# First router: additions between the statistics, the shared expert in front of each group's logits with a sigmoid, the first pair's missing weights spread by TensorE

## The reference, cut to what matters

```python
logits = x @ router_w.T + expert_bias[None, :]
probs = jax.nn.sigmoid(logits)
top_w, top_idx = jax.lax.top_k(probs, 8)
top_w = top_w / (jnp.sum(top_w, axis=-1, keepdims=True) + 1e-09) * 2.5
combine = zeros((T, 160)).at[arange(T)[:, None], top_idx].set(top_w)
h1 = jax.nn.silu(jnp.einsum('th,eih->eti', x, w_gate))
routed = jnp.einsum('eti,ehi->th', h1 * combine.T[:, :, None], w_down)
shared = jax.nn.silu(x @ w_gate_shared.T) @ w_down_shared.T
return routed + shared
```

## Time and profile before

| | us |
|---|---|
| median of 3 runs | 1087.96 |
| lowest and highest | 1087.72 and 1097.57 |
| the profiled execution | 1088.41 |
| its span in the trace | 1086.4 |
| PE, DVE, ACT, POOL busy | 1022.1, 821.4, 801.1, 227.5 |
| loop over heads ends, first mixture's loop starts | 316.2 and 365.2 |

### The profile page before, as it was taken

One profiled execution on the slowest core, in us unless ns is written; L12 is line 12 of the kernel. 1 busy time (PEld: TensorE's weight loads), 2 busy tenths in 40 slices (PEclk: granted clock), 3 DMA queues, 4 the chain that ended last, 5 costly groups with the idle time before them and its releaser, 6 DMA issues.

```text
span 1086.4 us, 20393 instructions
## 1 busy us (share of the span) xinstructions
PE 1022.1 (94%) x5232; PEld 692.5 (64%) x5264; DVE 821.4 (76%) x1954; ACT 801.1 (74%) x1326; POOL 227.5 (21%) x337
## 2 busy tenths in 40 slices
PE   5799999999987799999999999999999998799998
PEld 3333333333344588888888888888866777587786
DVE  8544444444439499999999999999986886799897
ACT  6699999999964677777777777888864443266664
POOL 3777764555452000000000000000023112000000
PEclk9999999999998999999999999999999998899999
DMA  4478787667650677777777777777720000223321
GB/s 139 127 234 263 242 258 227 215 228 229 223 169 5 223 257 248 242 241 242 240 242 234 247 239 242 241 241 238 236 73 1 1 1 1 81 86 117 122 81 39
DMA packets 103419, 190.51 MB, mean 175 GB/s; under 512 B 11980, under 2 KB 56652, under 8 KB 103372
## 3 DMA queue, kind: packets, MB, share of 16 engines
q1 hardware_dynamic: 103380, 190.06, 53.9%
HBM read 154.03 MB, written 35.98 MB: 175 GB/s over the span
## 4 chain that ended last, share of the span: by engine, by line
PE 84%; DVE 6%; ACT 3%; issue 2%; DMA 2%; POOL 2%; SPq 0%; DVEq 0%; ACTq 0%; POOLq 0%
PE bank L1348 27%; PE bank L1361 16%; PE bank L1203 11%; PE bank L1355 8%; PE bank L1184 6%; PE bank L1187 5%; PE bank L1450 2%; PE bank L1214 1%; PE bank L1434 1%; DVE xn L1541 1%; POOL m_norm L815 1%; DMA ring<-c_rows 1%; DVE stats L1529 1%; PE bank L1139 1%; ACT silu_z L1042 1%
## 5 line engine op out<-in xcount | busy, mean ns | idle before, releaser
L1348 PE MATMUL bank<-xh,w_parts 128*128 128x512 f32 x896 | 276.3, 390 | 1.6 <-DVEq L1757 1.6
L928 ACT ACTIVATE ring<-bank,minus_bound 128x1024 f32<-128x1024 f32 x256 | 262.8, 1119 | 9.2 <-DVE bank L1638 6.2
L1016 ACT ACTIVATE bank<-bank 128x512 f32<-128x512 f32 x320 | 186.2, 582 | 89.2 <-PE bank L1348 89.2
L1771 DVE TENSOR_TENSOR bank<-bank,ring 128x512 f32<-128x512 f32 x320 | 223.8, 699 | 27.8 <-DMA ring<-c_rows 2.9
L1361 PE MATMUL bank<-hh,w_parts 128*128 128x512 f32 x776 | 239.3, 389 | 0.0
L1763 DVE TENSOR_TENSOR hl<-bank,hh 128x512 fp32r<-128x512 f32 x321 | 218.2, 680 | 0.1
L1010 ACT ACTIVATE hh<-bank 128x512 fp32r<-128x512 f32 x321 | 190.5, 594 | 2.6 <-DVE bank L1771 2.4
L1348 PEld LDWEIGHTS bank<-xh,w_parts 128*128 128x128 f32 x896 | 167.4, 188 | 37.4 <-DVEq L1757 1.8
L1638 DVE TENSOR_TENSOR bank<-bank,corner 128x128 f32<-128x128 f32 x256 | 76.3, 298 | 151.8 <-PE bank L1187 149.3
L1348 PE MATMUL bank<-xl,w_parts 128*128 128x512 f32 x448 | 174.4, 389 | 0.0
L1361 PEld LDWEIGHTS bank<-hh,w_parts 128*128 128x128 f32 x776 | 145.6, 188 | 30.7 <-ACT hh L1010 0.4
(11 more groups left out here) (297 smaller groups left out, 1131.6 us busy)
## 6 DMA issues: line engine op xcount, KB each, us to landing
ring<-c_rows SPq DMA_DIRECT2D x176, 512.0 KB, 4.7
w_parts<-w_pairs SPq DMA_DIRECT2D x160, 128.0 KB, 2.9
w_pairs<-xh SPq DMA_DIRECT2D x16, 768.0 KB, 4.4
q_stack<-q_parts SPq DMA_DIRECT2D x64, 144.0 KB
k_stack<-k_parts SPq DMA_DIRECT2D x192, 48.0 KB
w_pairs<-xl SPq DMA_DIRECT2D x16, 512.0 KB, 2.9
big<-in_w_exp SPq DMA_DIRECT2D x16, 384.0 KB, 4.9
w_ffn_parts<-xl SPq DMA_DIRECT2D x16, 384.0 KB, 3.8
```

The source lines that it names most:

```text
L928: act.activation(ring[:, c % RING * S:(c % RING + 1) * S], wide[(m + c) % SB][:], ACT.Exp, bias=minus_bound[:]).then_inc(exp_done, 1)
L1016: act.activation(bank(4 + c % ZB), bank(4 + c % ZB), ACT.Silu).then_inc(silu_ready, 1)
L1348: ins = pe.matmul(out_, w[i], x_[j], start=start and k == 0, stop=stop and k == 2, skip_group_check=not start)
L1771: dve.tensor_tensor(bank(4 + c % ZB), bank(4 + c % ZB), cb[u][:, g * GW:(g + 1) * GW], ALU.mult).then_inc(hid_ready, 1)
```

## The change

It has four parts. PE's first two projections stand inside both branches of the If, ahead of its end. DVE adds a projection ahead of that group's statistics, and not all four first. The shared expert's first product stands ahead of each group's logits; ACT takes from it a copy (`shared_z`) and a sigmoid (`shared_hid`), and POOL multiplies the two, so that no Silu is left ahead of the loop; the four spare matmuls per group are gone, and the second product stands behind the first group's turned weights. For the last group DVE scales the weights, ACT copies both parts, and for the first pair of experts PE spreads the rows of tokens 1024 to 2047 with a matrix of ones and zeros (`pair_rows`), which ACT copies to the place that a load filled before.

```diff
--- before.py
+++ after.py
@@ -173,6 +173,7 @@
         b_rest = sb("b_rest", [P, NE])
         bias_rows = sb("bias_rows", [P, NE], F32R)
         ones_r = sb("ones_r", [P, P], F32R)
+        pair_rows = sb("pair_rows", [P, P])
         w_shared = sb("w_shared", [P, EI])
         wd_shared = sb("wd_shared", [EI, D])
         gates = big[:, 2 * T:2 * T + NT * NE].rearrange("p (t e) -> p t e", t=NT)
@@ -211,6 +212,7 @@
 
         act_out = [q_stack[0][u][:].bitcast(F32) for u in range(2)]
         shared_hid = act_out + [k_stack[0][u][:].bitcast(F32) for u in range(2)]
+        shared_z = [k_stack[1][u][:].bitcast(F32) for u in range(2)] + [evac[u][:] for u in range(2)]
         hid = [q_stack[1][u][:].bitcast(F32) for u in range(2)]
         hh = [sb(f"hh{u}", [P, GW], F32R) for u in range(2)]
         hl = [sb(f"hl{u}", [P, GW], F32R) for u in range(2)]
@@ -593,14 +597,13 @@
                 load_pair(u, u)
             for g in range(G):
                 cols = slice(g * GW, (g + 1) * GW)
-                sp.wait_ge(cT_ready, min(2 * g + 2, 2 * G - 1))
-                if g == G - 1:
-                    sp.wait_ge(cT_end, 1)
+                sp.wait_ge(cT_ready, 2 * g + 1)
                 sp.dma_start(c_dram[0:P, cols], cT_first[:, cols]).then_inc(c_saved, 16)
+                sp.wait_ge(cT_ready, 2 * g + 2)
                 sp.dma_start(c_dram[P:NE, cols], cT_last[:, cols]).then_inc(c_saved, 16)
                 if g % 2:
                     sp.wait_ge(c_saved, 2 * (g + 1) * 16)
-                    for u in range(2):
+                    for u in range(g // 2, 2):
                         load_rows(u, u, g // 2)
             for u in range(2, CB):
                 for h in range(2):
@@ -771,6 +774,9 @@
 
             pool.wait_ge(w1_loaded, 4 * 16)
             link(pool.tensor_copy(ones_r[:], ones[:]))
+            for e in range(2):
+                link.sign(pool.tensor_copy(pair_rows[:, e:P:2], across(ident[:, e:e + 1], EI)))
+            link.wait()
             link(pool.tensor_copy(b_part[0][:], b_router[:]))
             link(pool.tensor_tensor(b_rest[:], b_router[:], b_part[0][:].bitcast(F32), ALU.subtract))
             link(pool.tensor_copy(b_part[1][:], b_rest[:]))
@@ -786,6 +792,9 @@
             link(pool.memset(hid[1], 0.0))
             pool.sem_inc(moe_zero, 1)
             norm(1)
+            for g in range(G):
+                pool.wait_ge(shared_act, g + 1)
+                pool.tensor_tensor(shared_hid[g][0:EI], shared_hid[g][0:EI], shared_z[g][0:EI], ALU.mult).then_inc(shared_ready, 1)
             link(pool.memset(v_flat[:, 0:NT * 2 * B * NCH], 0.0))
             for h in range(2):
                 link.sign(pool.memset(half_column(h, 2, 0, NT), 1.0 / CH))
@@ -970,36 +979,42 @@
 
             def take_group(g):
 
+                act.wait_ge(shared_psum, g + 1)
+                act.activation(shared_z[g][0:EI], bank(2 + g % 2)[0:EI, :], ACT.Copy)
+                act.activation(shared_hid[g][0:EI], bank(2 + g % 2)[0:EI, :], ACT.Sigmoid).then_inc(shared_act, 1)
                 take_logits(g)
                 high_x(g, 1)
 
-            def take_shared(g):
-
-                act.wait_ge(shared_psum, g + 1)
-                act.activation(shared_hid[g][0:EI], bank(2 + g % 2)[0:EI, :], ACT.Silu).then_inc(shared_act, 1)
-
             act.wait_ge(w_saved[0], 16 + NH // 2 * 16)
+            act.wait_ge(moe_zero, 1)
             norm(1, take_group)
             take_group(G - 1)
-            act.wait_ge(moe_zero, 1)
 
             def take_cT(g):
 
                 cols = slice(g * GW, (g + 1) * GW)
                 act.wait_ge(cT_psum, g + 1)
                 act.activation(cT_first[:, cols], bank(4 + g % 2), ACT.Copy).then_inc(cT_ready, 1)
+                act.activation(cT_last[:, cols], bank(6 + g % 2)[0:NE - P, :], ACT.Copy).then_inc(cT_ready, 1)
+
+            def take_spread(k):
+
+                act.wait_ge(spread_psum, k + 1)
+                ins = act.activation(cb[0][:, (2 + k) * GW:(3 + k) * GW], bank(6), ACT.Copy)
+                if k == 0:
+                    ins.then_inc(spread_taken, 1)
+                else:
+                    ins.then_inc(cb_loaded[0], 16)
+
+            for g in range(G):
                 if g < G - 1:
-                    act.activation(cT_last[:, cols], bank(6 + g % 2)[0:NE - P, :], ACT.Copy).then_inc(cT_ready, 1)
-
-            for g in range(G):
-                if g < 2:
-                    take_shared(2 * g)
-                    take_shared(2 * g + 1)
-                act.wait_ge(combine_ready, g + 1)
-                for t in range(TPG):
-                    act.activation(rest[g][:, t, :], rest[g][:, t, :], ACT.Copy, scale=top_inv[:, g * TPG + t:g * TPG + t + 1])\
-                        .then_inc(scaled_ready, 1)
+                    act.wait_ge(combine_ready, g + 1)
+                    for t in range(TPG):
+                        act.activation(rest[g][:, t, :], rest[g][:, t, :], ACT.Copy, scale=top_inv[:, g * TPG + t:g * TPG + t + 1])\
+                            .then_inc(scaled_ready, 1)
                 take_cT(g)
+                if g >= 2:
+                    take_spread(g - 2)
             act.sem_inc(silu_ready, CREDIT)
             act.sem_inc(hh_ready, CREDIT - 1)
 
@@ -1151,6 +1166,16 @@
             pe.wait_ge(bound_root, 1)
             pe.matmul(bank(6)[:, 0:1], ones[0:1, :], bound[0:1, 1:2], start=True, stop=True).then_inc(bound_psum, 1)
 
+            def projection(g):
+
+                pe.wait_ge(oT_ready, g + 1)
+                if g >= 2:
+                    pe.wait_ge(x_ready, g - 1)
+                for t in range(TPG):
+                    ins = pe.matmul(bank(2 + g % 2)[:, t * P:(t + 1) * P], oT[:, g * GW + t * P:g * GW + (t + 1) * P], wo[:],
+                                    start=True, stop=True)
+                ins.then_inc(y_psum, 1)
+
             def turn_heads(g):
 
                 b, q0 = g // 2, (g % 2) * TPG
@@ -1234,6 +1259,8 @@
                 turn_heads(1)
                 for half_ in range(2):
                     turn(NH, 0, half_)
+                projection(0)
+                projection(1)
             with pe.Else():
                 pe.sem_inc(s_psum, CREDIT)
                 pe.sem_inc(prT_psum, CREDIT)
...
@@ -1311,33 +1328,47 @@
                 router_biases(g)
             def shared_hidden(g):
 
+                pe.wait_ge(x_ready, min(g + 3, G))
                 if g >= 2:
                     pe.wait_ge(shared_act, g - 1)
                 pe.matmul(bank(2 + g % 2)[0:EI, :], w_shared[:], xnT[:, g * GW:(g + 1) * GW], start=True, stop=True)\
                     .then_inc(shared_psum, 1)
 
-            norm(1, router_logits, 4)
-            pe.wait_ge(x_ready, G)
+            def tokens_of(g):
+
+                pe.wait_ge(xnT_ready, G + g + 1)
+                shared_hidden(g)
+                router_logits(g)
+
+            norm(1, tokens_of)
+            pe.wait_ge(gate_ready, G)
+
+            def spread(k):
+
+                pe.wait_ge(cT_ready, 2 * (2 + k) + 2)
+                pe.matmul(bank(6), pair_rows[:], cT_first[:, (2 + k) * GW:(3 + k) * GW], start=True, stop=True).then_inc(spread_psum, 1)
+
             for g in range(G):
-                if g < 2:
-                    shared_hidden(2 * g)
-                    shared_hidden(2 * g + 1)
-                if g == 0:
-                    pe.wait_ge(gate_ready, G)
-                if g == 2:
-                    pe.wait_ge(shared_act, G)
-                    for k in range(G):
-                        pe.matmul(bank(k), wd_shared[:], shared_hid[k][0:EI], start=True, stop=False, skip_group_check=True)
                 if g >= 2:
                     pe.wait_ge(cT_ready, 2 * (g - 1))
                 for t in range(TPG):
-                    pe.wait_ge(scaled_ready, g * TPG + t + 1)
+                    if g < G - 1:
+                        pe.wait_ge(scaled_ready, g * TPG + t + 1)
+                    elif t == 0:
+                        pe.wait_ge(combine_ready, G)
                     pe.transpose(bank(4 + g % 2)[:, t * P:(t + 1) * P], rest[g][:, t, 0:P], ident[:])
                     ins = pe.transpose(bank(6 + g % 2)[0:NE - P, t * P:(t + 1) * P], rest[g][:, t, P:NE], ident[:])
                 ins.then_inc(cT_psum, 1)
+                if g == 0:
+                    for k in range(G):
+                        pe.wait_ge(shared_ready, k + 1)
+                        pe.matmul(bank(k), wd_shared[:], shared_hid[k][0:EI], start=True, stop=False, skip_group_check=True)
+                if g == 2:
+                    spread(0)
+            pe.wait_ge(spread_taken, 1)
+            spread(1)
             pe.wait_ge(moe_zero, 1)
-            pe.wait_ge(cT_ready, 2 * G - 1)
-            pe.wait_ge(cT_end, 1)
+            pe.wait_ge(cT_ready, 2 * G)
             pe.wait_ge(xl_ready, G)
             for opened in (z_psum, down_done, low_used):
                 pe.sem_inc(opened, CREDIT)
@@ -1373,6 +1404,8 @@
```

(25 more changed lines are left out.)

16 lines of the change are left out of this document (5 added, 11 removed).

## The result

| | us |
|---|---|
| the changed kernel, median of 4 runs (lowest to highest) | 1123.37 (1121.34 to 1130.72) |
| the kernel before, median of 4 runs | 1089.47 (1087.72 to 1097.57) |
| ratio, with its 95% interval | 1.0305 (1.0269 to 1.0341) |
| the profiled execution of the changed kernel, its span | 1124.47, 1122.4 |

It is **slower by 3%**. The forecast was 1111.3, with 1101 to 1123 as range; the median lies 0.4 us above the range's upper end, 12.1 above the forecast. Two executions further down, one of loads_back (1299.29 us) and one of best (1687.51), had a far lower granted clock (0.745 and 0.558 as means) and are left out of their medians and ratios. The profiled execution is 36.0 us longer than that of before (spans 1122.4 and 1086.4).

What follows compares the result with a forecast made beforehand. PE was taken to bound the kernel, with 84% of the span. Router -9.4, removed stop -2.05 and table loads +34.8 made +23.3 on the profiled 1088.41, or 1111.8; less 0.45 for the median, 1111.3 us, range 1101 to 1123.

Steps and rivals of the forecast that it cites:

- Part 5: First mixture's loop: ACT's table load moves inside and runs in 40 turns, 0.87 us each, adding 34.8 us.
- Rivals 1 to 4: Table load: waits for PE's result (12%), costs less (14%), is skipped or hidden (4%), has a drain ahead (3%).
- its 1167: Kernel's end in us if the skill page's drain made each loop load cost PE about 1.4 us more.
- Part 4: Loop's first pair: PE's stop for a late load of weights goes, 2.05 us less.
- Parts 1 to 3: Router, from attention's end to the loop's start: the loop starts at 355.8, 9.4 us earlier.
- Part 1: Attention to router: projections ahead of the branch let DVE start early; PE turns the first group at about 326.3.
- Part 2: Router groups: cadence stays about 3.8 us; DVE comes last, ending at 347.3, 4.5 us earlier.
- Part 3: Turned weights to loop start: PE and ACT alternate for 13.8 us after ACT leaves its groups at about 341.0.
- Rival 5: Router gains nothing: without spare matmuls PE falls to 1.2 GHz in the groups, some 9 us, 1118 to 1121; 9%.

Runs made afterwards that it cites:

- loads_back: silu_ahead with the first pair's weights of tokens 1024 to 2047 loaded from memory, without the spread by PE and ACT: 1090.92 us, ratio 0.9985.
- best: all_together with the first two projections behind the If again and nine spare matmuls ahead of the second group: 1081.86 us, ratio 0.9921.
- two_loads: The changed kernel with a one-column Sigmoid ending each of ACT's 40 turns, so two table loads per turn: 1198.77 us, ratio 1.0982.
- silu_ahead: The changed kernel with a one-column Silu on ACT in a pause ahead of the loop, taking the table load there: 1089.63 us, ratio 0.9962.
- projections_back: silu_ahead with the first two projections behind the end of the If, as in the kernel before: 1089.55 us, ratio 0.9971.
- pool_late: all_together with POOL's four shared-expert products held until ACT has taken all four groups: one run of 1076.07 us, then median 1080.56, ratio 0.9901.
- spares_gap: silu_ahead with seven unread matmuls in PE's 1.72 us wait for the first group's scaled weights: 1083.30 us, ratio 0.9915.
- all_together: silu_ahead with shared second products spread over groups, seven plus six spare matmuls, and the last group turned ahead of both spreads: 1081.19 us, ratio 0.9891.

## Why the prediction was right and wrong

**Part 5, the table load, was right.** I derived from the order of instructions and the rows that a load moves into the loop, that it is executed although its set is active, and that it starts right behind `hh`. All 40 are there. The price was 0.93 and not 0.87. In the turn shown, the first product came 0.76 us late and the second 0.11 more, as the sum had it (0.75 and 0.11); the 0.06 that it lacks lie somewhere in the products behind them. That makes 37.4 and not 34.8, an error of 2.6 us. Silu came 1.03 late, as worked out. Rivals 1 to 4 are out: the load waits for no PE result, costs neither half nor double, has no drain ahead of it, and none is skipped. The prediction names the drain as one per switch, and these 40 loads switch nothing, so they alone could not decide on its 1167; two_loads has the real switches, and no drain either. The step that decided the sign was read from a mere eight loads in the second mixture and the place of one instruction in the code.

**Part 4 was right**: the stop for the load of c_rows is gone from the chain, and the loop with all 40 loads taken out (silu_ahead) is 2.3 us shorter than before (439.20 and 441.52), for a forecast of 2.05.

**Parts 1 to 3 were wrong: 9.4 us were to come and none came.** Counted from the last turned head, the loop was to start at 40.2 (355.8 - 315.58) and starts at 49.91. The 9.7 us divide so:

- *Part 1, 2.3 us.* "the branch and its 3.1 us come behind them" counted one stop; there are two. The first turned group comes at 13.04 and not at 10.7. By projections_back the second stop goes with the projections' place.
- *Part 2, 0.9 us.* A group takes 4.08 and not 3.8, and PE and ACT pace it. The logits take 1.35 and not 1.1: the pitch is the 0.14 of the sum, but the second follows the first after 0.24, and the last one's full length of 0.30 stands ahead of ACT's sigmoid. That POOL slows DVE beside it is true and costs nothing that pool_late could tell.
- *Part 3, 6.5 us.* From ACT's leaving the groups to the loop I had 14.8, and it took 21.3. The failed step is the sentence "where that was so before, the clock then was 1.2 GHz, which would add 1.6", of which I then counted only 1.0. I saw the pause, 1.72 in the end, and the lower clock behind it, but took from the trace of before how long it would last. It lasted from 346 to nearly 363. Counted in the same way, the stretch takes 16.1 in spares_gap, which only fills the pause, and 17.1 in projections_back, where the clock held through the products without that; silu_ahead, on which both are built, takes 21.0, so some 4 to 5 of the 6.5 us are the clock's. all_together takes 12.6, but it also has two alternations of PE and ACT fewer than the sum.

Rival 5 named the right mechanism, the clock without spare matmuls, with the right size (some 9 us in all, 1118 to 1121), but put it into the groups, where the clock stayed 1.0, and I gave it 9%. The forecast's loads and rival 5's router together are what happened: 1111.8 + 9.7 + 2.6 is 1124.1, against a profiled 1124.47; what is left are small terms in both directions (attention -0.4, part 4 -0.3, behind the loop +1.0). The direction was right for the reason given. That the median came within 0.4 of the range is owed to rivals 1 and 5, which its width took in, and not to the forecast's own sum.

Why the clock stayed down for 17 us in the changed kernel and for 3.4 before is not settled, and was not tried by itself, nor why the same pause took it down there and not in projections_back. One difference is what PE ran meanwhile: before, products of 128 rows (the shared expert's first), in the change mostly products of 64 rows and small turnings. That can't be all of it, since in projections_back the clock stayed down for 10.3 us under work of 128 rows. Nor is it shown what PE waits for in the stops at the end of the If; I only know where they stand.

## What to carry to other kernels

Before the last instruction of some function is taken out ahead of a loop, look at what its absence makes the compiler do inside it: here a table load in a loop that PE bounds cost 0.93 of its 1.28 us in every turn, and one dummy activation in a pause ahead of the loop removed them all. Spare matmuls whose result nobody reads are work: whoever takes them out has to ask what the clock will be in the stretch behind, over all of that stretch and not over the pause. And a saving ahead of a branch can come back as a stop behind it, as it did here.

## What had not been expected of the hardware

- A table load for the set that is already active takes the same 1.28 us as a real change of set, with 0.02 us around either (two_loads).
- Stops of 2.1 us in an otherwise full PE took the clock to 1.2 GHz in eight turns of 39, at 1.57 us each; stops of 0.6 never did.
- PE, busy without a gap from 344.4 to 354.5, stayed at 1.2 GHz (changed kernel).
- The same pause of 1.72 us was followed by a fall of the clock in six kernels and by none in projections_back.
- Code that was moved ahead of the end of an If turned one stop of about 3 us into two of 1.9 to 2.9.
- A DVE operation on 128x4 took 0.17 us alone and up to 0.93 beside a product of POOL.
